# The up weights of two expert stages laid out with four neighbouring rows to a partition, and the row transposes that go with it

## The reference

```python
# first one: 32 experts, 4 per token, F = 2 * 192
gate_up = einsum('TD,EDF->TEF', x, gate_up_proj)      # D = 512
g, u = split(gate_up, 2, axis=-1)
next_states = einsum('TEF,EFD->TED', u * silu(g), down_proj)
next_states = (next_states * router_weights[..., None]).sum(axis=1)

# second one: 32 routed experts (and 32 that do nothing), 8 per token, F = 2 * 256
gu = einsum('ech,ehf->ecf', buf, w_gate_up)           # h = 512, at most 256 rows an expert
g, u = split(gu, 2, axis=-1)
y = einsum('eci,eih->ech', silu(g) * u, w_down)
```

## Time and profile before

| | |
|---|---|
| median of 3 runs | 2188.98 us (2186.55 to 2194.15) |
| the profiled execution | 2185.58 us, of which the span is 2183.7 us |
| first experts, tiles 0 to 95, on TensorE | about 650 to 1130 us |
| second experts, tiles 0 to 63, on TensorE | about 1791 to 2163 us |
| TensorE busy over the span | 1827.7 us (84%) |
| VectorE busy | 1468.7 us (67%) |
| DMA | 271.46 MB in 202105 packets |

### The profile page before, as it was taken

One profiled execution on the slowest core, in us unless ns is written; L12 is line 12 of the kernel. 1 busy time (PEld: TensorE's weight loads), 2 busy tenths in 40 slices (PEclk: granted clock), 3 DMA queues, 4 the chain that ended last, 5 costly groups with the idle time before them and its releaser, 6 DMA issues. The chain is left out here.

```text
span 2183.7 us, 33673 instructions
## 1 busy us (share of the span) xinstructions
PE 1827.7 (84%) x9039; PEld 906.7 (42%) x9039; DVE 1468.7 (67%) x3127; ACT 1049.8 (48%) x1893; POOL 882.2 (40%) x949
## 2 busy tenths in 40 slices
PE   4689787998539999999973399999998539999997
PEld 2244443444425555555532033333332414445453
DVE  5887887779576665656546478888884765555554
ACT  5587877777422332333324066666666412222221
POOL 5476686666114555555533111111111013444442
PEclk8799988999759999999985599999999759999998
DMA  5101211111546889887646912111111717898994
GB/s 145 54 40 40 88 59 49 40 50 44 179 131 146 183 203 235 207 211 180 121 75 206 160 39 56 54 54 54 54 55 33 282 42 187 230 230 224 230 228 76
DMA packets 202105, 271.46 MB, mean 124 GB/s; under 512 B 83484, under 2 KB 121852, under 8 KB 200956
## 3 DMA queue, kind: packets, MB, share of 16 engines
q1 hardware_dynamic: 156315, 166.52, 25.3%
q0 software_dynamic: 38544, 97.02, 22.1%
q10 hardware_dynamic: 7121, 6.44, 1.7%
HBM read 200.25 MB, written 69.17 MB: 123 GB/s over the span
## 5 line engine op out<-in xcount | busy, mean ns | idle before, releaser
L2142 DVE TENSOR_REDUCE a_negmax<-a_m 128x1 f32<-128x512 f32 x512 | 340.5, 690 | 97.1 <-PE a_m L1992 94.1
L291 POOL TENSOR_TENSOR g_near<-g_mask,g_tb 128x512 f32<-128x512 f32 x256 | 322.6, 1281 | 99.3 <-DVE g_emin L545 98.5
L2091 ACT ACTIVATE a_prob<-a_s 128x1024 f32<-128x1024 f32 x256 | 260.7, 1021 | 124.1 <-PE a_s L2003 121.6
L1539 PE MATMUL f_gu_bank<-f_wgu,f_xT 128*128 x768 | 265.7, 489 | 2.9 <-ACT f_xT L1587 2.9
L374 PE MATMUL g_pt<-g_ident,g_p 128*128 128x128 f32 x1024 | 171.8, 297 | 93.0 <-DVE g_pT L554 87.7
L1501 POOL DMA_INDIRECT out<-f_y,f_ids x96 | 151.2, 1575 | 209.9 <-DMA out<-f_y,f_ids 167.2
L1992 PE MATMUL a_m<-a_kT,a_qT 112*128 (+1 forms) x512 | 204.5, 401 | 35.9 <-DMA a_kT<-a_one_rows 25.0
L1292 PE MATMUL s_gu_bank<-s_wgu,s_xT 128*128 128x512 f32 x512 | 232.5, 597 | 2.3 <-ACT s_xT L1344 1.6
L475 ACT ACTIVATE g_p<-g_e,g_emin 128x512 f32<-128x512 f32 x256 | 184.2, 720 | 96.8 <-DVE g_emin L545 96.3
L374 PEld LDWEIGHTS g_pt<-g_ident,g_p 128*128 128x128 f32 x1024 | 120.8, 149 | 222.9 <-DVE g_pT L554 152.5
L554 DVE COPY g_pT<-g_pt 128x512 f32<-128x512 f32 x256 | 175.6, 687 | 44.4 <-PE g_pt L374 43.1
(11 more groups left out here) (294 smaller groups left out, 2730.4 us busy)
## 6 DMA issues: line engine op xcount, KB each, us to landing
s_wgu<-in_L_ffn_w_gate_up SPq DMA_DIRECT2D x32, 1024.0 KB
f_wgu<-in_L_ffn_gate_up_proj SPq DMA_DIRECT2D x32, 768.0 KB
s_wd<-in_L_ffn_w_down SPq DMA_DIRECT2D x32, 512.0 KB
a_qT<-q_parts SPq DMA_DIRECT2D x217, 64.0 KB, 2.2
g_tb<-neighbours SPq DMA_DIRECT2D x8, 1536.0 KB, 7.9
f_wd<-in_L_ffn_down_proj SPq DMA_DIRECT2D x32, 384.0 KB
q_parts<-p_part SPq DMA_DIRECT2D x48, 128.0 KB, 2.3
g_tb<-neighbours SPq DMA_DIRECT2D x8, 512.0 KB, 4.4
```

What stands on the lines that cost most here:

```text
L291: pool.tensor_tensor(near[:, n % LAG, :], mask[slot][:, local % NT, :], t_all[k % SLOTS][:, local // NT, :], ALU.add).then_inc(near_ready, 1)
L1539: last = nc.tensor.matmul(gu_bank[j % TR][:, 0:F], xT[j % TR][:, c, :], wgu_flat[:, bass.ds(place_of[j] + c * F, F)], start=(c == 0), stop ...
L2091: nc.scalar.activation(prob[n][:, :, :], s_bank[n % RING][:, :, :], ACT.Exp).then_inc(p_ready, 1)
L2142: V.tensor_reduce(negmax[k % RING][:, st, head:head + 1], m_bank[n % RING][:, :], X_AXIS, ALU.max, negate=True).then_inc(m_read, 1)
```

## The change

Chunk c of partition p of `wgu` is now the row 4 * p + c of the expert's matrix, in all three places that load it. The four rows of a partition then lie side by side in DRAM, so each partition receives one contiguous piece of 4 * F floats: 6144 bytes in the first stage, 8192 in the second. The bytes and their place in `wgu` stay the same in number. To multiply the same features with each other, piece c of the transposes takes the columns c, c + 4, c + 8 and so on of a row in place of 128 neighbouring ones; in float32 the weight load then reads one element every 16 bytes. The down weights are loaded as before.

```diff
@@ route, SP @@
                 for e in range(RE):
-                    sp.dma_start(wgu[:, e, :, :], gate_up[e, :, :].rearrange("(c p) f -> p c f", p=P)).then_inc(wgu_in, 16)
+                    sp.dma_start(wgu[:, e, :, :], gate_up[e, :, :].rearrange("(p c) f -> p c f", p=P)).then_inc(wgu_in, 16)
@@ capped_experts and open_experts, SP @@
                     sp.dma_start(wgu[:, bass.ds(e % RE, 1), :, :].rearrange("p a c f -> p (a c) f"),
-                                 gate_up[bass.ds(e, 1), :, :].rearrange("a (c p) f -> p (a c) f", p=P)).then_inc(wgu_in, 16)
+                                 gate_up[bass.ds(e, 1), :, :].rearrange("a (p c) f -> p (a c) f", p=P)).then_inc(wgu_in, 16)
@@ capped_experts, turn @@
                     for c in range(DC):
-                        last = nc.tensor.transpose(xt_bank[k % TR][:, c, :], row[k][:, c * P:(c + 1) * P], ident[:, :])
+                        last = nc.tensor.transpose(xt_bank[k % TR][:, c, :], row[k][:, c:D:DC], ident[:, :])
@@ open_experts, turn @@
                     for c in range(DC):
-                        last = nc.tensor.transpose(xt_bank[j % TR][:, c, :], row[k][:, c * P:(c + 1) * P], ident[:, :])
+                        last = nc.tensor.transpose(xt_bank[j % TR][:, c, :], row[k][:, c:D:DC], ident[:, :])
```

## The result

The changed kernel takes 2197.44 us (median of 20 runs, 2189.05 to 2212.10), against 2187.00 us for the kernel before (20 runs, 2184.82 to 2194.15) on the same chip. The ratio is 1.0049, 95% interval 1.0040 to 1.0059: slower by half a per cent. Two later measurements, on other chips, gave 1.0028 (1.0016 to 1.0041) and 1.0035 (1.0017 to 1.0054), or 6.9 and 7.3 us between the medians. It is slower each time, and the size lies about 0.3 to 0.5%.

A forecast was written before the change was run, and what follows sets the result against it. TensorE's queue was taken to bound both expert stages. Strided load +1.3, transfer 0 and routing 0 gave 2188.98 + 1.3 = 2190.3 us, with a full range of 2184 to 2258 us and the forecast's own 2186 to 2193.

The forecast's parts named there:

- What bounds the kernel: Middle of both expert stages: TensorE is busy throughout, so lengthening its queue is paid in full, and relieving other engines gains nothing.
- Part 1: Row transposes of both expert stages: the strided weight load costs +1.3 us, with ends of 0 and +67.
- the router's row: Weight loads of the router's product: 111 ns for columns, spacing 0.112 us against 0.108, used to price a doubled load.
- three times: Row transposes: a load three times as long needs 175 ns, 0.067 us more each, or 43 us.
- upper bound of +67 us: Row transposes: a load four times as long, priced by the 0.213 us spacing at 1.2 GHz, for all 640.
- Part 2: Up weights' transfer: longer pieces relieve DMA engines by 0.7 us an expert, worth 0 in time, with ends 0 and -8.2.
- The routing at 0: Routing stages: earlier landing of the first four experts' weights shortens nothing; at most 3 us a stage without VectorE's cover.
- Rival 1: Four transposes of each tile: the load sticks out above 108 ns; +43 us at three times, +67 at four; chance 0.35.
- Rival 2: First expert stage: long weight pieces delay the results' scatters, then ScalarE and TensorE wait; +18 to +52 us, chance 0.05.
- Rivals 3 and 4: Weights' waits and routing relieved, 2175 us, chance 0.04; transfer still short pieces, packets 202105, 2190.3 us, within the forecast's 0.56.
- What would show it: Signs in the profile after: load medians, transposes to down product 0.43 to 0.45 us, rounds, packets, DMA share, scatter trails.
- The last sign: Expert stages: prediction wrong if load columns need over about 108 ns, or TensorE shows idle time mid-stage.

## Why the prediction was right or wrong

- **What bounds the kernel: right.** TensorE's queue sets the time of both stages, and what lengthened it was paid in full (7.2 us by the rounds, 7.2 by the stages), while what relieved the DMA engines was paid nothing.
- **Part 1, the strided load: the step that failed.** The model of the load held: the columns are 0.46 ns each beside a latency of 81 ns, and the load begins to cost from about 108 ns of columns. The size of the case that the forecast took was met as well: it has 117 ns for a doubled load, and the first of each four needs 116. What failed is the price of that case. The text called a load of 117 ns "still hidden", although its own limit is 108 and it puts that limit at 1.9 times of now. It priced it by the router's row (111 ns, 0.004 us, 2.6 us for all 640) and then took half of that, 0.002 us a transpose and +1.3 us. The doubled load costs 0.011 us, +7.2 us. The text's own way of pricing three times, columns less 108, would have given 117 - 108 = 9 ns and 5.8 us for twice. The router's row stands just where the price starts to rise, and five nanoseconds more made it almost three times as high. The upper bound of +67 us was far off; nothing here came near four times. (By columns less 108 that bound would have been 80 us; the 67 took the spacing of the low clock for it.)
- **The two statements of the Trainium skill.** The Trainium skill, "Advanced Engine Details and Errata", section Memory Cachelines, warns of a penalty for a different line at each access, and a penalty is what came. The measure that the Trainium skill gives in the same section, two hits in a line of 16 bytes, is not borne out by this load: two hits (step two, 209 ns) cost as much as one (step four, 210), and step three costs less (196). That a step of four float32 is free (the Trainium skill, "SBUF — State Buffer", section Door 1) does not hold for it: 140 became 210 ns.
- **Part 2, the transfer: right in the sum, off in a size.** The value of 0 was measured twice (0.9995, 0.9998), and the packets fell to 177529, against 177500. The relief was put at 0.7 us an expert. The queue's share of its engines is 24.9 to 25.3% in the kernels with short up weights and 23.9 to 24.5 in those with long ones. In the two profiles of the result that is 25.3% of 2183.7 less 23.9% of 2195.9, 27.7 us over 64 experts or 0.43 us each, and in the others it is less. The share of the DMA in the middle of the first stage was to be 0.77 and is 0.80; with the stride alone it is 0.81, so that figure hardly tells the two kernels apart.
- **The routing at 0: right.** With the transfer alone the routing stages are 0.2 and 0.4 us shorter up to their first up product, which is nothing beside the 3 us a stage that stood as the bound.
- **Rival 1: right in its place, its mechanism and its threshold (116 ns lies above 108), wrong in its price.** It was given +43 at the least, because the prediction knew no case between "twice, hidden" and "three times". At twice it is +7. The chances of 0.56 for no change and 0.40 for slower thus rested on a gap between two cases, and the result fell into it: 7.2 us by the rounds, just above the 6.6 us taken as the limit of no change. The range held the time, but only because it reached up to the price of a load four times as long, which never came; the forecast's own range of 2186 to 2193 did not hold it.
- **Rival 2: not seen as described, but its premise named the wrong thing.** The slack was taken from the buffers of `y` (16.5 us beyond a trail of 8.6). What is late first are the gathered rows, in the profiles whose longest trail is 13 to 14 us, since the gathers stand behind the scatters on GpSimd. The trail of 20 us never came.
- **Rivals 3 and 4:** neither occurred (no kernel with the long pieces was measurably faster, and the packets fell).
- **What would show it:** "about 200 a doubling, 260 and more rival 1" left 210 at the doubling, which was to cost 2.6 us at the most; "the distance must stay 0.43 to 0.45" caught it, at 0.48. The last sign, "wrong if the load's columns need more than about 108 ns", gave the right answer too.

## What to carry to other kernels

Where short matmuls follow each other, the weight load beside each has a slack that can be read off the trace (here the matmul's spacing of 108 ns less 58 ns of columns), and the case to price first is the one just beyond it, not the far bound. When several such loads stand in a row, take the length from the first, since the records of the others may hold waiting. Count every matmul that has such a load: 640 times 11 ns was more than 24576 packets fewer could give back, because the queue they left was not the one that TensorE waited for. A load that sticks out can be hidden by setting it beside a long matmul, if that order costs less than it saves.

## What the runs showed of the hardware

- A weight load of 128 columns of float32 (four transposes in a row, 2.4 GHz) takes 137 ns with a step of zero, 140 with one, 209 with two, 196 with three, 210 with four (medians). The first of the four takes 137, 141, 195, 193 and 197. At 1.2 GHz the first takes 183 with a step of one and 196 with four.
- Beside matmuls of 128 columns at 2.4 GHz, first loads of 193, 195 and 197 ns lengthen the spacing of some 0.109 us by 0.005, 0.010 and 0.011 us. Beside matmuls of 512 columns the load of 197 ns lengthens nothing.
- Read with a step of four float32, a 128x512 activation on ScalarE took 1314 ns in place of 811, and a tensor_scalar on VectorE 745 in place of 544.
- Pieces of 6 KB in place of 1.5 KB (in the second stage 8 KB in place of 2), a quarter as many for the same bytes, lowered the queue's share of 16 engines' time from about 25.1% to about 24.3%, and the kernel's time by nothing that could be measured.
